# A causal attention kernel on eight cores: the projection groups of the next head pair move to later key steps, and an activation reload is waited for in quarters

## What is computed

```python
# x: (4, 2048, 2048), 16 heads of 128, all float32
qkv = einsum('bsd,de->bse', x, W_qkv)            # W_qkv: 2048 x 6144
attn = softmax(q @ k.T / sqrt(128) + alibi + causal_mask)
y = (attn @ v) @ W_o
x = layernorm(x + y)
h = silu(x @ rw1.T + rb1); logits = (h @ rw2.T + rb2)[:, :16] + gates
coeff = softmax over the top 2 of logits, 0 elsewhere
out = x @ W.T + bias + sum over experts of ((x @ A.T) * coeff) @ B   # rank 16
x = layernorm(x + out)
```

## Time and profile before

| | us |
|---|---|
| median of two runs | 5351.92 (5333.15 and 5370.69) |
| profiled execution | 4960.06 |
| its span on the slowest core (core 2) | 4958.5 |
| spans of the eight cores | 4942.6 to 4958.5 |
| mean granted TensorE clock, every core | 0.934 to 0.936 |
| TensorE matmul busy | 4275.5 (86%) |
| VectorE, ScalarE busy | 785.7, 357.4 |

### The profile page before, as it was taken

The page is one execution under the profiler, slowest core; times in us unless marked ns, Lnnn a source line. Parts: engine busy times, 40 slices in busy tenths (PEclk is TensorE's granted clock), DMA queues, the critical chain, the costliest instruction groups (busy, mean ns, idle before and its releaser), DMA issues.

```text
span 4958.5 us, 39203 instructions; the slowest of 8 cores (4942.6 to 4958.5 us)
## 1 busy us (share of the span) xinstructions
PE 4275.5 (86%) x15336; PEld 2938.6 (59%) x15336; DVE 785.7 (16%) x1312; ACT 357.4 (7%) x595; POOL 46.5 (1%) x88
## 2 busy tenths in 40 slices
PE   7788899998999989989989989976999745888882
PEld 6677787785776767767857757732443324333330
DVE  0000001112112111111121121131000142111115
ACT  0000000001001011011011010120000000000000
POOL 0000000000000000000000000000000000000000
PEclk9899899999999999989999999988999967999996
DMA  5221234232232232332323322123111001000001
GB/s 164 74 77 55 88 96 140 82 106 81 95 113 79 82 121 63 107 101 82 112 76 100 108 79 82 58 86 118 51 49 42 26 22 34 26 26 26 26 17 68
DMA packets 373492, 376.47 MB, mean 76 GB/s; under 512 B 18624, under 2 KB 336192, under 8 KB 373056
## 3 DMA queue, kind: packets, MB, share of 16 engines
q1 hardware_dynamic: 326656, 264.90, 17.7%
q10 hardware_dynamic: 39168, 83.90, 5.6%
q0 software_dynamic: 7488, 25.17, 1.3%
HBM read 348.75 MB, written 25.17 MB: 75 GB/s over the span
## 4 chain that ended last, share of the span: by engine, by line
PE 81%; DVE 8%; DMA 7%; issue 2%; SPq 1%; ACT 1%; DVEq 0%; ACTq 0%; POOL 0%; POOLq 0%
PE bank L314 18%; PE bank L290 18%; PE bank L517 9%; PE bank L958 9%; PE bank L681 9%; PE bank L355 4%; PE bank L364 4%; PE bank L407 4%; DMA posb<-alibid 4%; DMA qh<-wqkv 1%; PE bank L873 1%; DVE st_sb L462 1%; DVE st_sb L442 1%; PE bank L973 1%; SPq L108 1%
## 5 line engine op out<-in xcount | busy, mean ns | idle before, releaser
L314 PE MATMUL bank<-wv,xb 128*128 128x256 f32 x4096 | 905.3, 381 | 0.0
L290 PE MATMUL bank<-xb,wk 128*128 128x256 f32 x4096 | 900.5, 379 | 0.0
L314 PEld LDWEIGHTS bank<-wv,xb 128*128 128x128 f32 x4096 | 783.1, 191 | 124.5 <-issue 17.3
L290 PEld LDWEIGHTS bank<-xb,wk 128*128 128x128 f32 x4096 | 775.6, 190 | 114.5 <-issue 3.3
L681 PE MATMUL bank<-yfm_all,wocol 128*128 128x512 f32 x1024 | 447.3, 595 | 31.4 <-DMA yfm_all<-y_hbm 31.4
L958 PE MATMUL bank<-x1fm,wtcol 128*128 128x512 f32 x1024 | 448.8, 596 | 13.8 <-DMA bP_sb<-bP 13.8
L355 PE MATMUL bank<-pt_sb,V 128*128 128x512 f32 (+3 forms) x768 | 339.5, 526 | 103.1 <-ACT pt_sb L450 102.9
L407 PE MATMUL bank<-qh,K 128*128 128x512 f32 (+3 forms) x768 | 332.4, 544 | 75.7 <-DMA qh<-q_hbm 43.9
L681 PEld LDWEIGHTS bank<-yfm_all,wocol 128*128 128x128 f32 x1024 | 195.4, 191 | 277.8 <-issue 277.8
L958 PEld LDWEIGHTS bank<-x1fm,wtcol 128*128 128x128 f32 x1024 | 197.3, 193 | 264.9 <-issue 264.9
L364 PE MATMUL bank<-pt_sb,ones_sb 128*128 128x512 f32 (+3 forms) x768 | 326.2, 508 | 0.0
(11 more groups left out here) (83 smaller groups left out, 1596.9 us busy)
## 6 DMA issues: line engine op xcount, KB each, us to landing
xb<-xT SPq DMA_DIRECT2D x256, 512.0 KB, 6.9
qh<-wqkv SPq DMA_DIRECT2D x64, 256.0 KB, 6.9
wk<-wqkv SPq DMA_DIRECT2D x32, 512.0 KB, 10.9
posb<-wqkv SPq DMA_DIRECT2D x64, 256.0 KB, 4.8
wv<-wqkv SPq DMA_DIRECT2D x32, 512.0 KB, 8.6
posb<-alibid ACTq DMA_DIRECT2D x32, 512.0 KB, 4.3
wocol<-wo SPq DMA_DIRECT2D x64, 256.0 KB, 4.3
wtcol<-wT SPq DMA_DIRECT2D x64, 256.0 KB, 3.9
```

Of the source, the lines that this page charges most:

```text
L290: mmk = p.op("tensor", (lambda bi_, fc_, oc_, tb_, par_: (lambda e: e.matmul(banks[bi_][:, 0:256], wk_sb[par_][:, fc_ * 256 + oc_ * 128: f ...
L314: mmk = p.op("tensor", (lambda bi_, fc_, tt_, tb_, par_: (lambda e: e.matmul(banks[bi_][:, 0:256], xb[tb_ % 2][:, fc_ * 256 + tt_ * 128: f ...
```

## The change

Two things are changed.

First, where the steps of `kv_gen` are called. Before, head 0 of a pair calls two steps at each of `kc` 0 and 1 and one at each of `kc` 2 to 15 (18 steps: four of loads, 14 groups), and head 1 calls two at each of `kc` 0 to 8 (18 groups). After, head 0 calls one step at `kc` 4, 6, 8 and 10 (the four load steps) and one at each of `kc` 12 to 15 (4 groups), and head 1 calls two at each of `kc` 0 to 13 (28 groups).

Second, each of the eight 1 MB DMAs of `y_hbm` gets a buffer record and a semaphore of its own, the two halves are loaded alternately, and the matmuls wait for the quarter that they read, four feature blocks at a time, instead of for a whole half.

```diff
@@ attention @@
                             if hd2 == 0:
-                                if kc < 2:
+                                if kc in (4, 6, 8, 10) or kc >= 12:
                                     next(gen, None)
-                                    next(gen, None)
-                                else:
-                                    next(gen, None)
-                            elif kc < 9:
+                            elif kc < 14:
                                 next(gen, None)
                                 next(gen, None)
@@ output projection @@
-                ymk_h = []
-                for th in range(2):
-                    mk = yball[th].load(
-                        [dap(yfm_all, fc0 * 1024 + th * 512,
-                             [[FCN * 1024, 128], [1024, 4], [1, 512]])
-                         for fc0 in range(0, FCN, 4)],
-                        [dap(y_hbm, fc0 * 128 * OWN + th * 512,
-                             [[OWN, 128], [128 * OWN, 4], [1, 512]])
-                         for fc0 in range(0, FCN, 4)], split=4)
-                    ymk_h.append(mk)
+                yb8 = [[B("sync") for _ in range(4)] for _ in range(2)]
+                ymk_p = [[None] * 4 for _ in range(2)]
+                for gp in range(4):
+                    for th in range(2):
+                        fc0 = 4 * gp
+                        ymk_p[th][gp] = yb8[th][gp].load(
+                            dap(yfm_all, fc0 * 1024 + th * 512,
+                                [[FCN * 1024, 128], [1024, 4], [1, 512]]),
+                            dap(y_hbm, fc0 * 128 * OWN + th * 512,
+                                [[OWN, 128], [128 * OWN, 4], [1, 512]]))
...
-                        p.wait("tensor", ymk_h[tb])
                         for fc in range(FCN):
+                            p.wait("tensor", ymk_p[tb][fc // 4])
...
-                        yball[tb].use(mmk)
```

## The result

| | before | after |
|---|---|---|
| median of all runs, us | 4971.27 (11 runs, 4961.28 to 5561.46) | 5002.56 (12 runs, 4982.26 to 5555.18) |
| ratio to before | | 1.0055 (95% interval 1.0037 to 1.0073) |
| profiled execution, its slowest span | 4960.06, 4958.5 (core 2) | 4991.29, 4988.5 (core 4) |
| from the first bias addition of pair 0 to that of pair 7 | 2434.4 | 2460.8 |

The change makes the kernel 0.55% slower; a gain of 0.34% was forecast. Some executions of either kernel are disturbed and take up to 12% longer, and the two runs shown ahead of the prediction were both of that kind; so the median of 5352 to which the forecast was scaled was no base for it, and 5334 with its range missed the level of the result by 330 us. On the base of the profiled execution the forecast was 4943 us and the measured 4991.

What follows compares the result with a forecast made beforehand. TensorE's matmuls, 86% of the span, were taken as the bound. Attention -18 us and y reload +1 made -17: 4943 of 4960.06 us, scaled to 5334 on the 5351.92 median; own range 5310 to 5360, overall 5280 to 5390.

Steps and rivals of the forecast that it cites:

- The load steps: Moving the `xb`, `wk`, `wv` load steps to `kc` 4 to 10 in head 0 costs nothing; loads are issued long before use.
- Bare steps of head 0: Head 0, steps 2 to 11 without groups: 38.3 us instead of 34.4, so 3.9 us lost per pair.
- (b): Rival: bias loads of bare steps land late, 1 us for each of nine steps, 63 us in all; 13%.
- (c): Rival: TensorE falls to the low clock in bare wide steps, 213 us slower; 4%.
- The bare tail: Last group's copy to the pair's ending store: 36.6 to 18.7 us in pairs 0 to 5, 31.2 to 14.9 in pair 6.
- the collision: In tails of pairs 0 to 5, the second `xb` load delays step 14's 64 KB bias load by 3.8 us.
- Rival (a): Tail collision gone or small, the 64 KB bias load slips through: another 23 us gained, y stage at its best; 15%.
- The joints: Between heads and pairs, `qh` load, reciprocals and first QK are untouched; difference 0.
- the three signs: Wrong if bare-step bias loads exceed 4 us, tails keep 25 us or more, or bare-step 512-column matmuls take 2.05 a pair.
- The reload of y: Reload of y after the attention: TensorE starts 10 us earlier but awaits the seventh landing; net +1 us, bounds -2.4 and +3.9.
- The cold last quarter: In the y reload, the last quarter's matmuls run at the low clock after a gap, giving +1 us.
- Rival (d): If the longer runs have slower matmuls, the 3.9 us bare-step waits disappear under them: 27 us more gain; 10%.

Runs made afterwards that it cites:

- hold_joint: Changed kernel, but SyncE holds the `xb` load of token block 2 until head 1's `qh` load has landed; slowest span 4959.6 us (before 4958.5).
- hold_both: `hold_joint` with the next pair's block 1 `xb` load also held until that pair's `qh` has landed; 0.9982 of before (0.9969 to 0.9995).

## Why the prediction was wrong

**The load steps**: right. The order on the SP queue did not change, and the first waits of TensorE name no `xb`, `wk` or `wv`.

**Bare steps of head 0**: right in kind, a little small. Timeline of TensorE in pair 5 after, the first and the last row of the stretch:

```profile
2582.36 1.67 PE L407 MATMUL bank<-qh,K 128*128 128x512 f32 x4
...
2621.16 0.59 PE L407 MATMUL bank<-qh,K 128*128 128x256 f32 x2
```

A window over the same stretch, columns as in the earlier trace rows:

```profile
2582.00:2621.10 39.10, 36.13 (x102) 18.00 (x101) 10.24 (x15) 12.48 (x19) 0.00 (x0) 1.00 0.29 82
```

2621.16 - 2582.36 = 38.8 us, forecast 38.3 (pair 7), clock 1.00; the seven pairs take 38.2 to 39.7. Rivals (b) and (c) did not come. By the additions head 0 cost 32.7 us over seven pairs, 27.3 forecast.

**The bare tail**: right in kind. The gain was 39.1 us instead of 45.3. The sum took 3.8 us for the collision, and it was 4.8: in the rows above, and as a mean of pairs 0 to 5, where additions 13 to 15 take 9.8 us and those of pair 6 before 5.0. From the last copy to the store tails 0 to 5 take 19.7 us (18.7 forecast); pair 6 came as forecast, from the last copy at 3253.20 to the store at 3268.43, 15.2 us against 14.9. Rival (a), a small load that slips through, did not come: the load of a quarter of the size was delayed as long.

**The joints**: this step failed. "The joints between heads and pairs (`qh` load, reciprocals, first QK) are untouched" was true of the instructions and false of what runs beside them. It is 30.7 of the 44.4 us between the forecast sum of -18.0 and the measured +26.4; the rest is 6.2 in the tail, 5.4 in the bare steps and 2.1 at the joint of pairs. The middles' waits for `qh` went from 17.9 to 48.9 us, the whole of the 30.7, and holding one load gave 29.7 of it back (`hold_joint`). None of the three signs by which the prediction said it would be wrong concerned the joints. Even with them untouched the gain would have been a quarter of the forecast: `hold_joint` shows 4.5 us in pairs 0 to 6, not 18. The prediction had the rule in hand: it counted four groups to a block, priced the collision of an `xb` load at the tail, and did not ask where else a block now ends. The row to look at was the load of `qh` in the earlier trace rows.

**The reload of y**: the quarters came as forecast, the clock did not. TensorE after:

```profile
3423.06 6.20 PE L678 MATMUL bank<-yfm_all,wocol 128*128 128x512 f32 x8 [21.92 <-DMA yfm_all<-y_hbm]
3429.61 3.67 PE L678 MATMUL bank<-yfm_all,wocol 128*128 128x512 f32 x8 [0.35 <-DMA yfm_all<-y_hbm]
3436.36 3.67 PE L678 MATMUL bank<-yfm_all,wocol 128*128 128x512 f32 x8 [3.07 <-DMA yfm_all<-y_hbm]
3442.41 3.67 PE L678 MATMUL bank<-yfm_all,wocol 128*128 128x512 f32 x8 [2.38 <-DMA yfm_all<-y_hbm]
3447.10 1.10 PE L700 MATMUL bank<-x1fm,ones_sb 128*128 128x512 f32 x2 [1.01 <-DVE x1fm L692]
```

The first quarter runs mostly at the low level (granted clock 0.59 over it); behind gaps of 3.07 and 2.38 us the last ones take 3.67 at 1.00. So the stage gained 3.0 us (a loss of 1 forecast, at best a gain of 2.4). The cold last quarter did not come, and the seventh landing came 28.8 us behind the first issue instead of 29.7. The prediction drew on the Trainium skill's page "TensorE: Matmul & The Clock Gate", section "HAM oscillation — how this bites in real kernels", and let every quarter start cold by it; one quarter of four did. The section's example has waits for DMA of about 3 to 5 us ahead of each tile, and the gaps here, 0.35, 3.07 and 2.38 us, lie below or at the short end of that, so this case neither bears the rule out nor contradicts it.

**The scale**: a second miss, of the number alone: moving the result to the median of two runs 8% above the profiled execution put the number outside the level of the profiles. The range contained only the level of those two, although the profiled execution itself lay 320 us below its lower end. Rival (d), that slower runs gain more, was not tested.

## What to carry to other kernels

When work is moved within an engine's stream, list the DMAs that its last use of a buffer releases, and look which exposed load is issued within a few microseconds of each new release point; a schedule of groups that ends on a multiple of the buffer's period puts the two together. If a small load waits at a joint, issue it earlier into its free buffer before tuning what fills the joint: here that was worth about 1.2% of the kernel after for `qh` alone (0.9939 against 1.0055 of before) and 2.4% of the kernel before for `qh` and the bias loads together, the new filling nothing. Ask of each joint which wait ends last: early `qh` did nothing where VectorE waits for a store. And a base for the forecast should be taken from the same execution as the rows.

## What the runs showed that I had not expected

A 512 KB `qh` load takes 5.8 to 9.7 us to land when 2 MB of `xb` are issued 1 us ahead of it, and 3.3 to 3.8 otherwise (middles of after, core 4, and of before, core 2). A 64 KB bias load is delayed beside `xb` by 3.5 to 4.9 us and a 256 KB one by 3.5 to 4.2: the delay does not shrink with the small transfer. Two cores of a die can be granted 0.81 for at least 100 us while the other two run the same matmuls at 1.00; the span of the slower of them was 27 us above the highest of the other six. A load held on a queue until an exposed one has landed gave back 15.4 of the 24.4 us that it gained (means of eight cores of `hold_both`), since it landed beside the next exposed one.
